# Sending the choice of experts through DRAM as a row to all partitions, and making the masks from it by comparison

## The reference, cut to what matters

```python
x = x + xattn(layernorm(x), ctx, ctx)
t = rmsnorm(layernorm(x)) * norm_w
probs = softmax(t @ gate_w.T)                  # 8 experts
topw, topi = top_k(probs, 2); topw = topw / sum(topw)
h1 = t @ w1.T + 2 * (t @ a1[e].T) @ b1[e].T    # e = each of the two chosen experts
h3 = t @ w3.T + 2 * (t @ a3[e].T) @ b3[e].T
act = silu(h1) * h3
out_e = act @ w2.T + 2 * (act @ a2[e].T) @ b2[e].T
x = x + sum over the two e of topw[e] * out_e
```

## Time and profile before

| | |
|---|---|
| median of three runs | 319.68 us |
| profiled execution | 318.86 us, span 316.8 us |
| granted PE clock, mean | 0.989 |
| PE busy | 300.6 us, 95% of the span |
| DVE busy | 224.4 us, 71% |
| ACT busy | 198.2 us, 63% |
| POOL busy | 189.2 us, 60% |
| bytes moved | 8.95 MB, 28 GB/s in the mean |

### The profile page before, as it was taken

How to read it: one execution, slowest core, us unless ns; L and a number is a source line. 1 busy time by engine, 2 the same in 40 slices (tenths; PEclk the granted TensorE clock), 3 DMA queues, 4 the chain that set the end, 5 groups by cost and what they waited for, 6 DMA issues and landing times. The chain is left out here.

```text
span 316.8 us, 4667 instructions
## 1 busy us (share of the span) xinstructions
PE 300.6 (95%) x1569; PEld 243.6 (77%) x1569; DVE 224.4 (71%) x621; ACT 198.2 (63%) x337; POOL 189.2 (60%) x171
## 2 busy tenths in 40 slices
PE   6778999999999999999999999999999999998994
PEld 5546787768787888888887888888887878786873
DVE  3767984895669756895769756895669756963375
ACT  2456956478647777478647767478747746863521
POOL 3363459927991588627892588717861489226920
PEclk9997999999999999999999999999999999999997
DMA  5720020000200020000200020000000000000000
GB/s 158 273 59 10 1 66 2 1 0 3 99 0 2 0 66 36 0 3 0 86 15 2 0 68 33 0 2 1 5 30 0 1 2 34 1 2 0 33 0 33
DMA packets 5063, 8.95 MB, mean 28 GB/s; under 512 B 560, under 2 KB 1840, under 8 KB 5040
## 3 DMA queue, kind: packets, MB, share of 16 engines
q1 hardware_dynamic: 4320, 7.54, 7.3%
q10 hardware_dynamic: 720, 1.12, 1.0%
HBM read 6.56 MB, written 2.10 MB: 27 GB/s over the span
## 5 line engine op out<-in xcount | busy, mean ns | idle before, releaser
L849 ACT ACTIVATE silu<-h_ps 128x512 f32<-128x512 f32 x64 | 38.2, 597 | 28.2 <-PE h_ps L573 26.2
L1131 DVE TENSOR_TENSOR act_first<-silu,h_ps 128x512 f32<-128x512 f32 x32 | 21.9, 686 | 42.1 <-ACT silu L849 25.1
L573 PE MATMUL h_ps<-um_hi,b_hi 128*128 128x512 f32 x128 | 51.3, 401 | 0.1
L573 PE MATMUL h_ps<-um_lo,b_hi 128*128 128x512 f32 x128 | 50.7, 396 | 0.1
L573 PE MATMUL h_ps<-um_hi,b_lo 128*128 128x512 f32 x128 | 50.6, 395 | 0.0
L1354 POOL TENSOR_TENSOR heads<-e_o,rec_o 128x512 f32<-128x512 f32 (+1 forms) x9 | 14.8, 1645 | 45.0 <-DVE rec_o L1040 45.0
L1383 POOL TENSOR_TENSOR scaled<-act_second,ratio 128x512 f32<-128x512 f32 x24 | 31.3, 1308 | 17.0 <-DVE act_second L1131 16.8
L1131 DVE TENSOR_TENSOR act_second<-silu,h_ps 128x512 f32<-128x512 f32 x32 | 21.3, 683 | 14.6 <-PE h_ps L573 13.8
L573 PEld LDWEIGHTS h_ps<-um_lo,b_hi 128*128 128x128 f32 x128 | 24.0, 188 | 6.2 <-DVE um_lo L1229 0.6
L573 PEld LDWEIGHTS h_ps<-um_hi,b_hi 128*128 128x128 f32 x128 | 24.1, 188 | 5.8 <-DVE act_first L1131 0.4
L573 PEld LDWEIGHTS h_ps<-um_hi,b_lo 128*128 128x128 f32 x128 | 24.1, 189 | 5.4
(11 more groups left out here) (273 smaller groups left out, 810.4 us busy)
## 6 DMA issues: line engine op xcount, KB each, us to landing
x_in<-in_x_dram SPq DMA_DIRECT2D x7, 256.0 KB, 2.9
ctx_in<-in_ctx_t_dram SPq DMA_DIRECT2D x7, 256.0 KB, 3.2
out_dram<-y SPq DMA_DIRECT2D x7, 256.0 KB, 2.0
act_second<-in_hidden_w_dram SPq DMA_DIRECT2D x1, 512.0 KB, 6.1
act_second<-in_lora_w_dram ACTq DMA_DIRECT2D x1, 512.0 KB, 6.0
v_parts<-in_down_w_dram SPq DMA_DIRECT2D x1, 512.0 KB, 5.8
attn_sb<-in_attn_w_dram SPq DMA_DIRECT2D x1, 260.5 KB, 5.7
ctx_in<-in_ctx_t_dram ACTq DMA_DIRECT2D x2, 128.0 KB, 4.4
```

The source lines that it names most:

```text
L573: mm = nc.tensor.matmul((h1_ps, h3_ps)[s][n % 2][:], b13[w][:, s, c * P:(c + 1) * P], um[k][m][:, s, :], start=False, stop=(i == 2), skip_ ...
L849: nc.scalar.activation(silu[:, n % SILU_RING, :], h1_ps[n % 2][:], ACT.Silu).then_inc(silu_done.sem, 1)
L1131: nc.vector.tensor_tensor((act_first, act_second)[k][:, c, :], silu[:, n % SILU_RING, :], h3_ps[n % 2][:], ALU.mult).then_inc(act_done.sem, 1)
```

## The change

For blocks 1 to 7 the one-hot, spread and turn stages go. Block 0 keeps them.

- DVE's `choose(n)` stands where `top_gap(n)` was: 4 `max_index`, the gap, and a cast of the two indices, all written into a tile `choice` of 12 numbers per token row (4 tiles times: first index, second index, gap).
- SP's `spread_choice(n)`, behind `store`, writes `choice` (128 rows of 48 bytes) to DRAM, waits for it, and reads all 1536 numbers back to each of the 128 partitions (`chosen`, 6 KB per partition, 768 KB in all).
- DVE's `mask(n, k)` compares `chosen` with the number of the expert that a partition belongs to. The reads step over 12 numbers (48 bytes) from token to token. The second one compares and subtracts the first mask.
- ACT's `exp_ratio(n)` takes exp of the gaps in `chosen`, also in steps of 48 bytes, straight into `ratio`. `spread_onehot`, `mask` and `ratio_turned` go from ACT, `spread_masks` and `turn_ratio` from PE.
- The factor 2 moves from the masks into `mask_u` and `v_part`, which become scalar_tensor_tensor with an immediate.
- The loops are written out by block, each weight has its own semaphore, and some waits move into the functions that need them. POOL's `low(B13)` no longer waits for `onehots`. The load of b13 moves from ACT's queue to SP's. In the last block `w2_product(LAST, 2)` now stands ahead of the last two `a2_product`.

```diff
+            def spread_choice(n):
+                sp.wait_ge(choice_done.sem, choice_done.of(n))
+                sp.dma_start(choice_dram[n % 2].rearrange("(p c) -> p c", c=CHOICE), choice[:])\
+                    .then_inc(choice_out.sem, 16)
+                sp.wait_ge(choice_out.sem, choice_out.of(n))
+                if n > 1:
+                    sp.wait_ge(masks_done.sem, masks_done.of(n - 1))
+                    sp.wait_ge(ratio_done.sem, ratio_done.of(n - 1))
+                sp.dma_start(chosen[:], choice_dram[n % 2].partition_broadcast(P)).then_inc(chosen_in.sem, 16)
...
-            def spread_masks(n):
-                for k in range(TOP):
-                    pe.wait_ge(silu_done.sem, silu_done.of(n - 1, 7 + k))
-                    pe.wait_ge(spread_done.sem, spread_done.of(n, k + 1))
-                    by_tile(h1_ps[k], lambda t: spread[:, k, t].rearrange("p e r -> p (e r)"),
-                            lambda t: ident_bf[:]).then_inc(masks_mm.sem, 1)
...
+            def exp_ratio(n):
+                sc.wait_ge(chosen_in.sem, chosen_in.of(n))
+                sc.wait_ge(scaled_done.sem, scaled_done.of(n - 1))
+                sc.wait_ge(scaled_last.sem, scaled_last.of(n - 1))
+                sc.wait_ge(mask_scaled.sem, mask_scaled.of(n - 1))
+                nc.scalar.activation(tile4(ratio), chosen_part(TOP), ACT.Exp).then_inc(ratio_done.sem, 1)
...
+            def choose(n):
                 ve.wait_ge(top_l_done.sem, top_l_done.of(n))
+                for t in range(TILES):
+                    op = nc.vector.max_index(top_i[:, t, :], top_l[:, t, :], logits[:, t, :])
+                op.then_inc(top_i_done.sem, 1)
...
+                nc.vector.tensor_tensor(choice[:, TOP * TILES:], top_l[:, :, 1], top_l[:, :, 0], ALU.subtract)\
+                    .then_inc(gap_done.sem, 1)
+                ve.wait_ge(gap_done.sem, gap_done.of(n))
+                ve.wait_ge(top_i_done.sem, top_i_done.of(n))
+                nc.vector.tensor_copy(choice[:, 0:TOP * TILES].rearrange("p (k t) -> p t k", k=TOP), top_i[:, :, 0:TOP])\
+                    .then_inc(choice_done.sem, 1)
+
+            def mask(n, k):
+                ve.wait_ge(chosen_in.sem, chosen_in.of(n))
+                dst = masks[n % 2][:, k, :].rearrange("p (t c) -> p t c", t=TILES)
+                if k == 0:
+                    ve.wait_ge(row_expert_in, 16)
+                    nc.vector.tensor_scalar(dst, chosen_part(0), row_expert_sb[:, 0:1], None, ALU.is_equal)\
+                        .then_inc(masks_done.sem, 1)
+                else:
+                    ve.wait_ge(masks_done.sem, masks_done.of(n, 1))
+                    first = masks[n % 2][:, 0, :].rearrange("p (t c) -> p t c", t=TILES)
+                    nc.vector.scalar_tensor_tensor(out=dst, in0=chosen_part(1), scalar=row_expert_sb[:, 0:1], in1=first,
+                                                   op0=ALU.is_equal, op1=ALU.subtract).then_inc(masks_done.sem, 1)
```

More of the change, by code:

```diff
@@ new lines, in _ @@
+            hidden(0, 7)
+            a2_product(0, 0, 1)
+            a2_product(0, 0, 0)
+            a2_product(0, 1, 1)
+            a2_product(0, 1, 0)
+            w2_product(0, 0)
+            w2_product(0, 1)
+            lora_in(1, 0)
+            lora_in(1, 1)
+            a2_product(0, 2, 1)
+            a2_product(0, 2, 0)
+            w2_product(0, 2)
+            a2_product(0, 3, 1)
+            a2_product(0, 3, 0)
+            w2_product(0, 3)
+            for b in range(1, LAST):
+                early = b + 2 < BLOCKS
@@ new lines, in _ @@
+            ctx_high(3)
+            silu_step(0, 6)
+            silu_step(0, 7)
+            b_high(0, 1)
+            b_high(0, 2)
+            z_high(0, 1)
+            z_high(0, 2)
+            exp_gap(1)
+            exp_ratio(1)
+            exp_o(2)
+            um_high(1, 0)
+            um_high(1, 1)
+            for b in range(1, LAST):
+                early = b + 2 < BLOCKS
+                silu_step(b, 0)
+                heads_turned(b + 1)
+                if early:
+                    normal_x(b + 2)
+                silu_step(b, 1)
+                v_high(b - 1)
+                if early:
+                    x_turned(b + 2)
+                silu_step(b, 2)
+                output_t(b - 1)
+                silu_step(b, 3)
+                normal_tok(b + 1)
@@ L1314, in _ @@
+            b_low(LAST, 2)
+            z_low(LAST, 1)
+            z_low(LAST, 2)
+            last_part(0, 0)
+            last_part(1, 0)
+            last_sum(0)
+            last_part(0, 1)
+            last_part(1, 1)
+            last_sum(1)
+            last_low(0)
+            last_low(1)
+            last_finish(0)
+            last_finish(1)
         @block.gpsimd
@@ L1445, in _ @@
                     norm_heads(b + 2)
-                if late:
-                    um_low(b + 1)
+                um_low(b + 1)
+            scale_mask(LAST)
+            v_sum(LAST - 1)
+            v_low(LAST - 1)
+            scale_step(LAST, 0)
+            scale_step(LAST, 1)
+            total_first(LAST)
+            b_low(LAST)
+            z_low(LAST)
+            scale_step(LAST, 2)
 _OUT = "out_dram"
```

656 lines of the change are left out of this document (396 added, 260 removed).

## The result

The changed kernel took 325.4 us in the median (322.72 to 326.14, 4 runs), the kernel before 320.45 beside it (318.21 to 324.47). The ratio is 1.0169, with a 95% interval of 1.0089 to 1.0249. A second comparison (E11) gave 1.0194, 1.0138 to 1.0249; the ratios leave out executions over 1.5% above the fastest of the same kernel, as the profiled one of E11 with 329.99 us. So the change makes this kernel slower, by 0.9 to 2.5%, with 1.7 and 1.9% as the two middle values. The forecast was 323.2 us, the range 317.5 to 330.

The account below looks back on a forecast made before the run. PE was taken as the bound in the mean, with the chain DVE, ACT, POOL 0.58 us away; 0.8 + 1.4 + 0.6 + 0.7 + 0.1 + 0.7 = +4.3 us on 318.86 gave 323.2 us, range 317.5 to 330.

Parts of the forecast that it names:

- Start: At the start, DVE's tok may wait up to 2.4 us for POOL's b_lo: +0.8 us, between 0 and +1.
- Block 0 to 1: Masks add 1.85 us, only some 0.4 of DVE's saving counts, and there is no margin: +1.4 us.
- Four steady blocks: Four blocks where PE took v_lo without waiting, each 0.16 us longer: +0.6 us.
- Sixth block: No margin before PE takes v_lo there: +0.7 us.
- Last block: DVE has less to do and the second mask partly falls into a wait for ACT: +0.1 us, between 0 and 0.7.
- End: Six 256-column matmuls of w2_product(LAST, 2) now stand ahead of the last a2_product, for which DVE waits: +0.7 us.
- Masks: Two DVE mask instructions ahead of um_low: 0.65 us for the first, 1.2 for the second, together 1.85 us.
- Search off the chain: Index search and one-hots leave DVE's chain, the search filling a wait before the fifth activation product: 1.11 us saved.
- Steady block: PE wants v_lo 0.95 us earlier, gets it 0.74 later: it waits 1.11 us, the block becomes 0.16 longer.
- the three places named in the prediction: PE's waits at um_lo (third low-rank matmul), the h3 half and v_lo, about 1.1 us together per steady block.
- the margin of 0.58: In a steady block, POOL's v_lo ends at 151.10 and PE takes it at 151.68: 0.58 us to spare.
- Transfer: Choice through DRAM: write 2.0 us, read 4.4 us, landed at 134.9, needed at 137.0, 2.1 us to spare.

Follow-up runs that it names:

- E11: The changed kernel itself, compared once more with the kernel before in five rounds: ratio 1.0194 (1.0138 to 1.0249).
- E1: Changed kernel plus four matmuls of 512 columns per block on PE, results unused, in blocks 0 to 6: 1.0155 of the kernel before.
- E2: Changed kernel with DVE's first mask instruction issued twice, once into a tile nobody reads: 1.0387 of the kernel before.
- E4: Changed kernel with the choice written to DRAM in 1536 pieces of 4 bytes, so each mask's 512 numbers lie side by side: 1.1566 of the kernel before.
- E3: Changed kernel with index search, gap and cast put back behind the fifth activation product: 1.0445 of the kernel before.
- E10: E9 with PE's b2 product of the block before behind hidden step 3 and ACT's output copy moved later: 316.12 us, 0.9911 of the kernel before.
- E7: Changed kernel with PE turning the choice, written as 12 rows of 512 bytes, so masks read side by side: 322.29 us, 1.0081 of the kernel before.
- E9: Changed kernel with E7's turned choice, E5's two ends, and gap and cast on POOL in block 6 alone: 321.56 us, 1.0038 of the kernel before.
- E5: Changed kernel with w2_product(LAST, 2) behind the last a2 products and POOL's b_lo waiting for the one-hots again: one execution, 328.82 us.

## Why the prediction was right, and where it was not

The mechanism was the forecast's: PE's 6.3 us come off, and the chain DVE, ACT, POOL takes them all (E1, E2). The size was a little low: 1.1 to 1.3% forecast, 1.7 and 1.9% measured. And the near agreement of the two profiles' 4.1 us with the predicted 4.3 is in part luck, since the term of the start (+0.8) is too large and those of the last block and the end (+0.8 together) are too small. By the ruler, the 4.1 us divide as follows.

| Term | Predicted | Measured | From |
|---|---|---|---|
| Start | +0.8 | -0.3 | first `umf`, 31.04 to 30.77 |
| Block 0 to 1 | +1.4 | +1.2 | mark 80.00 to 80.89, less the above |
| Four steady blocks | +0.6 | +0.3 | 223.27 to 224.46 |
| Sixth block | +0.7 | +0.55 | 258.62 to 260.36 |
| Last block | +0.1 | +1.2 | 289.82 to 292.74 |
| End | +0.7 | +1.2 | 316.8 to 320.9 |

**Masks.** 0.74 + 1.07 against 0.65 + 1.2: right in sum, and each within 0.13. The reason given for the second was wrong. I put it beside `scaled`, 1317 ns, as "two tensors from SBUF". But `um_lo` reads two tensors from SBUF as well and takes 1.16 us for 1024, 0.58 per 512. `scaled` is long because it runs beside POOL's own `scaled`: in block 6 of the changed kernel, where POOL's is all but over, it takes 0.69. Of the mask's 1.16 us, 0.42 are its steps (E4). The number came out by luck, and the row that would have spoken against my reason was among those I showed.

**Search off the chain.** 1.11 measured between the fifth product and `z_lo`, 0.9 when put back (E3).

**Steady block.** The chain to `um_lo` grew by 0.52 us (142.10 - 129.84 against 140.67 - 128.93), not 0.74: 1.81 for the masks, less 1.11, less 0.18 between the first `umf` and `sum_exp` and in waits for PE. PE lost 1.04 us per block, 35.90 against the 34.86 that its work alone needs (E10's 34.97 less the turn), where I had 1.11. It is lost in the three places named in the prediction: the starts of neighbouring matmuls lie 0.37 us further apart than the usual 0.23 ahead of the one that takes `um_lo`, 0.36 behind it, ahead of the h3 half, and PE idles 0.31 for `v_lo`. Two errors nearly cancel here. The chain grew by 0.5 us and not by 0.74, and PE starts 0.15 us after `v_lo` has ended (151.22 + 1.29 = 152.51, against 152.66), which the margin of 0.58 left out: 0.50 - 0.58 + 0.15 = 0.07 for the block, where the ruler shows 0.10 and the prediction had 0.16.

**Transfer.** 3.9 us for the read (4.4 taken), 1.6 for the write (2.0): landed at 134.8, due at 137.9. All partitions reading one row of 6 KB is no burden here. The bound for the write, that 6 KB can't take longer than a store of 256 KB (2.0 us), was a wrong argument with a right number: 6 KB in 4-byte pieces took 10.7 us (E4).

**Start.** `tok` did wait for POOL, 2.62 us instead of 0.60, and PE waited 0.47 us for it. From `tok`'s first half to the first `t_lo` pass 6.03 us, 5.27 before: +0.76. But most of that does not reach the chain. E7 and E9 differ at the start only in where `b_lo` stands, and had nearly the same clock there (0.93 from 24 to 28 us in both, 0.64 and 0.65 from 28 to 32). With `b_lo` back behind the one-hots `tok` takes 0.60 again, and the way to the first `t_lo` is 5.44 instead of 6.04 us, but the way to the first `umf` 11.67 instead of 11.77. So 0.1 us is gained, by an estimate 0.4 at most, not 0.8 (E9's clock from 20 to 24 us was 0.93 and E7's 1.00, which can hide 0.3 us): this term was sized wrongly. The -0.3 of the profiled pair is made of two parts. The changed kernel's first `tok` stands 0.44 us earlier (19.56 against 20.00), for a reason that no run isolates. From there to the first `umf` it takes 0.17 us more than the kernel before (11.21 against 11.04), which had a clock of 0.83 and 0.74 from 24 to 32 us, where the changed one had 1.00. With such differences between executions 4.1 us is one reading and the 5.0 at equal mean clock (E11) another; the first is likely too little.

**Last block.** This step of the prediction failed. I had written "between 0 and 0.7, I take 0.1", with the mask in a wait for ACT. That came true: `um_lo` follows the mask at once, where before it waited 1.12 us. What I missed is the search: moved ahead of the fifth product, gap lands 0.08 us behind the start of POOL's `z_lo` and stands there for 2.33 us, so that block 6 doesn't get the 1.11 us which the steady blocks got. By the prediction's own words, that it is wrong if the fifth product waits for the choice, it was wrong in this block. E9, which takes the two instructions off DVE there, needs 1.14 us less than E7 for block 6 to 7 (32.38 against 33.52), with the same late read. The prediction had this risk ("the cast waits behind POOL's next instruction, up to 0.7 us") but for the steady blocks, where it doesn't happen, and with too low a price: the price is the rest of POOL's product, up to 2.3 us. In block 0 the same happened to the cast, but DVE waits for POOL's `scaled` behind it anyway (2.62 us), and nothing was lost.

**End.** 0.69 us for the order of the products, 0.7 predicted, and E5 takes it back. Of the other 0.5, 0.14 lie on DVE between the first `v_parts` and the b2 products (2.96 us against 2.82, in E5 too), and 0.39 behind them, where the clock was at the lower level from the b2 products on, in the kernel before only behind them. The changed order, with its longer wait, may make that likelier, but it doesn't bring it each time (E5 has the count). Neither part was in the prediction.

## What to carry to other kernels

Before work is taken off the busiest engine, read how early the last input of each of its steps arrives; here it was 0.58 us with 0.95 to save, and the saving came back as waits, while the engine's busy time fell as planned. After a step is moved, look for what POOL is doing at the new place in every kind of block, first and last ones too: a DVE instruction of 4 columns took 2.3 us where POOL's product had started a moment before it. And give numbers that are read 512 wide side by side in memory; a turn on PE and 12 rows of 512 bytes pay for that, 1536 pieces of 4 bytes don't.
